# New instruction lists and PSUM banks for all five engines of a two-layer transformer kernel

## The chip, the core and the metric

The kernel runs on one core of one Trainium2 chip. A core has five engines that run their own instruction lists at the same time: PE (TensorE, matmuls), DVE (VectorE), ACT (ScalarE), POOL (GpSimd) and SP (SyncE, which here only starts DMAs). They meet through semaphores alone. The metric is the device time of one execution in microseconds (us); lower is better.

## What is computed

Two pre-norm transformer layers on `x` of 8 x 512 x 128 in float32. Each layer is attention and then a mixture of experts, each with a layernorm before it and a residual around it. Cut to its core:

```
x = x + attn0(layernorm(x))   # 16 heads of 8, 4 kv heads, causal softmax, @ wo.T
x = x + ffn0(layernorm(x))    # softmax over 8 experts, the best one: (silu(a) * g) @ w2[e], [a, g] = x @ w1[e], times its probability
x = x + attn1(layernorm(x))   # 16 heads of 8, k and v out of a normed latent of 32, rope on q and k, causal
x = x + ffn1(layernorm(x))    # softmax over 8 experts, the best two: relu(x @ w1[e] + b1[e]) @ w2[e] + b2[e], times their probabilities
```

## The kernel before

**Steps.** The function `all_steps` breaks the work into steps that carry a kind, a layer, a batch or group, and two numbers. Each step is a handful of instructions on one engine or on several. The kinds that matter here, in the order of one batch:

- Attention: `turn` (L1145, PE turns the normed rows), `lat`, `lat_turn`, `v1`, `rotate` (layer 1: latent, keys, values, rope), `park` and `stacks` (SP moves keys and queries into stacks), `max` (PE L1213 and L1219 compute scores for the row maximum, DVE L1524 reduces them to `neg_max`), `m_hi` (PE L1227 turns `neg_max`), `score` (PE L1239, then ACT L1453 takes the exponential and POOL L1088 masks), `values` (PE L1257), `normalise` (DVE L1637 and L1521 make `ctx_n`; PE L1267), `turn_ctx` (PE L1275), `project` (PE L1283).
- Routing: `logits` (PE L1292), `route` and `choose` (DVE, ACT), `places` (PE L1300 and L1301, then a chain of small DVE operations that count each token's place in its expert's rows), `scatter` (POOL L1099, an indirect DMA that puts the rows of a token block into `sorted_in`).
- Experts: `fetch` (SP L972 and L976, sorted rows into `rows_in`, two buffers), `turn_rows` (PE L1308), `fetch_w1` (SP L943, one load of weights for each tile of 128 rows, a ring of six in layer 1), `first` (PE L1331, ACT L1490), `second` (PE L1341, DVE L1521), and then in layer 0 a store to `sorted_out` and `combine` (POOL gathers, DVE L1797 adds to X), in layer 1 `send` (POOL L1107, an indirect DMA to `returned`), `take_back` (SP L997, two DMAs for a batch), `add` (DVE L1555, ACT L1499, POOL) and `store` (SP L1007). `tail` (SP L952) fills the ends of the last half's experts with empty rows. `load_expert` (SP L917) brings weights of the second matmul.

**Groups.** Layer 0 routes in two groups of four batches. Layer 1 has group 0 (batches 0 to 3, the first half) and groups 1, 2 and 3 (batches 4 and 5, 6, 7: the second half). The expert work of a group is mixed into the attention of later batches where there is any; the last burst of expert work runs from about 780 us to the end.

**What sets the order.** Nothing is scheduled at run time. `ORDERS` holds one string for each engine, one letter for each step in which the engine takes part; `Plan.read_orders` turns letters to steps, the n-th letter of a kind being its n-th step. Each engine then runs `for s in plan.order(...)` and waits, at each instruction, on the semaphore that says its input is there or its buffer free. So an instruction that waits holds all that stands behind it in its engine's list. `BANKS` gives, in the order of PE's list, the PSUM bank of each step that takes one: one digit each, with large steps on a pair of banks. Before, only the digits 0, 2, 4, 6 and 7 stand in it. A step waits until the last user of its bank has been read (`room(u)`).

**Rules that the change's steps touch.** `take_back` of a half starts with a wait for all its sends:

```
if x == rooms(1, g)[0]:
    for slot, value in enumerate(sends_made(of_half(1, half_of(1, g))[-1])):
        sp.wait_ge(sent_back[slot], value)
```

`fetch_w1` number n of layer 1 waits until the matmuls of `second` number n-6 have been read from PSUM. `fetch` number q waits for `turn_rows` number q-2. POOL puts a small operation and a wait for it (`pause`, L1032) after every second indirect DMA.

## Time and profile before

| what | value |
| --- | --- |
| runs, us | 958.96, 962.04, 961.92; median 961.92 |
| the profiled execution, us | 958.88, of it 957.0 between first and last instruction |
| granted TensorE clock, mean | 0.963 |
| PE busy | 856.2 us (89%) |
| DVE, ACT, POOL busy | 669.4, 609.4, 533.2 us |
| moved by DMA | 141.14 MB, mean 147 GB/s |

One execution was profiled. A line of the profile gives the start, the length, the engine, the line of the source, the tile written and the tiles read, and in brackets the idle time ahead of it with what ended it. `PE 89%` is an average: there are stretches of attention, in which PE and DVE are both nearly full, and bursts of expert work, in which DVE has little to do. A granted clock of 1.00 is TensorE at its full 2.4 GHz, 0.50 at 1.2 GHz. An `SPq` line is a stretch in which SP issued DMAs, their waits in it.

### The profile page before, as it was taken

What the parts mean: (1) busy time and instruction counts of PE and PEld (TensorE: products, weight loads), DVE (VectorE), ACT (ScalarE), POOL (GpSimd) and SP (SyncE); (2) the same over time, 40 slices, a digit from 0 to 9 for tenths busy, and PEclk for the clock granted to TensorE, in tenths of its full rate; (3) what the DMA queues carried; (4) which work ended last, traced back from release to release, by engine and by line L of the source; (5) the groups of instructions that cost most, each with busy time, mean ns of one, the idle gap of its engine ahead of it and who ended that gap; (6) DMA issues with size and microseconds to landing.
All of it is one profiled execution on the core that took longest, in us unless ns stands there. A gap on an engine that the chain in (4) does not pass through costs nothing.

```text
span 957.0 us, 24622 instructions
## 1 busy us (share of the span) xinstructions
PE 856.2 (89%) x8968; PEld 572.6 (60%) x8968; DVE 669.4 (70%) x1379; ACT 609.4 (64%) x1173; POOL 533.2 (56%) x809
## 2 busy tenths in 40 slices
PE   3689999989999899988999999999799997899991
PEld 1334455434999445434998444454445597799990
DVE  1889899788545899887567899789999537111117
ACT  3077889865444588685434696788578864555661
POOL 3043544557000588677203787567788775687452
PEclk9999999989999899979999999799899999999996
DMA  5625642444674436341984517435441256778786
GB/s 142 155 83 128 172 112 75 74 113 148 197 223 147 118 113 156 87 135 54 304 255 129 130 54 160 128 78 120 122 124 36 77 167 184 227 228 252 237 247 207
DMA packets 137312, 141.14 MB, mean 147 GB/s; under 512 B 35564, under 2 KB 113452, under 8 KB 137100
## 3 DMA queue, kind: packets, MB, share of 16 engines
q1 hardware_dynamic: 130604, 126.04, 47.4%
q0 software_dynamic: 6592, 13.55, 4.4%
q8 instruction: 74, 1.21, 0.5%
q14 instruction: 42, 0.34, 0.1%
HBM read 98.73 MB, written 44.36 MB: 150 GB/s over the span
## 4 chain that ended last, share of the span: by engine, by line
PE 36%; DVE 9%; issue 3%; DMA 2%; ACT 2%; SPq 0%; POOL 0%; DVEq 0%; ACTq 0%; POOLq 0%
PE psum L1331 11%; PE psum L1341 9%; PE psum L1257 5%; DVE neg_max L1524 4%; PE psum L1239 2%; PE psum L1213 2%; DMA rows_in<-sorted_in 1%; ACT scratch L1453 1%; PE psum L1308 1%; PE psum L1219 1%; PE psum L1283 1%; DVE route L1521 1%; PE psum L1175 1%; DVE X L1555 1%; DMA w<-sorted_out,rows_of 1%
## 5 line engine op out<-in xcount | busy, mean ns | idle before, releaser
L1524 DVE TENSOR_REDUCE neg_max<-psum 128x2 f32<-128x768 f32 (+3 forms) x352 | 379.6, 1119 | 41.0 <-PE psum L1219 38.7
L1453 ACT ACTIVATE scratch<-psum 128x1024 f32<-128x1024 f32 x320 | 316.1, 1022 | 80.4 <-PE psum L1239 77.9
L1088 POOL TENSOR_SCALAR_AFFINE_SELECT scratch<-scratch 128x512 f32<-128x512 f32 x256 | 158.5, 641 | 124.3 <-ACT scratch L1453 123.2
L1331 PE MATMUL psum<-rows_t,w_now 128*128 128x128 f32 x1360 | 169.5, 277 | 5.9 <-issue 3.8
L1257 PE MATMUL psum<-scratch,values 128*32 128x512 f32 (+3 forms) x2048 | 170.0, 452 | 1.7 <-POOL scratch L1088 0.8
L1331 PEld LDWEIGHTS psum<-rows_t,w_now 128*128 128x128 f32 x1360 | 159.7, 193 | 10.4 <-issue 7.4
L1213 PE MATMUL psum<-k_stack,q_stack 52*128 52x128 bf16 (+3 forms) x1024 | 133.2, 321 | 17.8 <-DVE neg_max L1524 7.9
L1341 PE MATMUL psum<-w,hidden_t 128*128 x992 | 131.3, 279 | 5.1 <-ACT hidden_t L1490 1.7
L1239 PE MATMUL psum<-q_stack,k_stack 55*128 55x512 bf16 (+3 forms) x1024 | 121.9, 312 | 12.7 <-DVE neg_max L1524 7.1
L1490 ACT ACTIVATE hidden_t<-psum,w_now 128x128 f32<-128x128 f32 x312 | 88.6, 373 | 60.6 <-PE psum L1331 46.3
L1341 PEld LDWEIGHTS psum<-w,hidden_t 128*128 128x128 f32 x992 | 119.7, 193 | 10.2 <-issue 10.0
L1099 POOL DMA_INDIRECT sorted_in<-xn_half,rows_of x96 | 94.1, 980 | 33.4 <-issue 20.8
L1213 PEld LDWEIGHTS psum<-k_stack,q_stack 52*128 52x128 bf16 x1024 | 43.8, 98 | 96.1 <-issue 39.0
L1521 DVE TENSOR_TENSOR w<-psum,w_now 128x128 f32<-128x128 f32 x78 | 22.7, 291 | 109.1 <-PE psum L1341 107.8
L1107 POOL DMA_INDIRECT returned<-w,goes_to x78 | 76.8, 985 | 37.9 <-issue 19.0
L1219 PE MATMUL psum<-masks_bf 64*128 64x64 bf16 (+2 forms) x1408 | 93.0, 211 | 0.0
L1257 PEld LDWEIGHTS psum<-scratch,values 128*32 128x32 f32 x2048 | 55.1, 111 | 62.1 <-issue 40.6
L1219 PEld LDWEIGHTS psum<-masks_bf 64*128 64x128 bf16 x1408 | 70.6, 101 | 30.9 <-issue 4.9
L1239 PEld LDWEIGHTS psum<-q_stack,k_stack 55*128 55x128 bf16 x1024 | 36.4, 96 | 73.1 <-issue 31.7
L1778 DVE SCALAR_TENSOR_TENSOR hidden_t<-w,psum 128x512 f32<-128x512 f32 x46 | 31.6, 687 | 58.2 <-PE psum L1341 33.0
L1070 POOL TENSOR_TENSOR rot<-rot 128x512 f32<-128x512 f32 x16 | 20.4, 1272 | 50.0 <-DVE rot L1521 49.9
L1078 POOL TENSOR_TENSOR max_parts<-max_rest,max_parts 32x128 bf16<-32x128 f32 x32 | 13.5, 422 | 57.3 <-ACT max_parts L1349 57.1
(141 smaller groups left out, 1007.2 us busy)
## 6 DMA issues: line engine op xcount, KB each, us to landing
w_now<-in_w SPq DMA_DIRECT2D x78, 322.0 KB
w_now<-in_w SPq DMA_DIRECT2D x46, 512.0 KB, 4.4
q_stack<-q_parts SPq DMA_DIRECT2D x64, 192.0 KB, 4.2
q_parts<-q_parts SPq DMA_DIRECT2D x16, 384.0 KB, 2.9
k_stack<-k_parts SPq DMA_DIRECT2D x32, 192.0 KB, 3.7
q_parts<-q_parts SPq DMA_DIRECT2D x16, 256.0 KB, 2.9
w<-in_w SPq DMA_DIRECT2D x16, 256.0 KB, 4.4
scratch<-returned SPq DMA_DIRECT2D x16, 256.0 KB, 4.0
```

Source lines behind the costliest of these rows:

```text
L1088: pool.affine_select(out=diag, in_=diag, compare_op=ALU.is_ge, fill=0.0, base=0, pattern=[[0, 4], [1, P]], channel_multiplier=-1).then_inc ...
L1099: pool.indirect_dma_start(sorted_in[s.layer][half_of(s.layer, g)][:, :], bass.IndirectOffsetOnAxis(ap=row_of(s.layer, g, t, k), axis=0), x ...
L1107: pool.indirect_dma_start(returned[h][:, :], bass.IndirectOffsetOnAxis(ap=goes_to[h][:, j:j + 1], axis=0), kept[slot], None).then_inc(sent ...
L1213: pe.matmul(out[:, j * width:(j + 1) * width], q_stack[i][rows, pair, t * P:(t + 1) * P], k_stack[i][rows, k_of(layer, pair), 0:width], st ...
L1219: ins = pe.matmul(blocks, ident_of[half, :], mask[half, :].unsqueeze(1).to_broadcast([P // 2, n, P // 2]), start=False, stop=(first > widt ...
L1239: ins = pe.matmul(bank[u.bank + k][:, off:off + SEQ - j * P], k_stack[i][rows, k_of(layer, pair), j * P:(j + 1) * P], q_stack[i][rows, pai ...
L1257: ins = pe.matmul(bank[u.bank][CW * c:CW * c + CW, j * P:SEQ], values[batch_of(s) % 3][:, j, col:col + CW], p[:, c % 2, off:off + SEQ - j ...
L1331: ins = pe.matmul(bank[v.bank][:, c * P:(c + 1) * P], w1_now[layer][w.slot][:, n * FFN + c * P:n * FFN + (c + 1) * P], rows)
L1341: ins = pe.matmul(bank[u.bank][:, 0:P], hidden_t[h.slot][:, k * P:(k + 1) * P], w2[layer][:, bass.ds(e, 1), k * DIM:(k + 1) * DIM].rearran ...
L1453: act.activation(expd[s.slot], psum[:, u.bank:u.bank + 2, :], ACT.Exp, scale=SCALE).then_inc(read[u.bank], 1)
L1490: ins = act.activation(hidden_t[s.slot][:, c * P:(c + 1) * P], bank[u.bank][:, c * P:(c + 1) * P], ACT.Relu, bias=w[:, FFN + c:FFN + c + 1])
L1524: return dve.tensor_reduce(out=out, in_=in_, axis=AX, op=op, negate=negate)
```

## The change

The strings of `ORDERS` are replaced for all five engines, and so is `BANKS`, in which 1, 3 and 5 now stand too. The steps are the same and so is the work of each. Since a `rotate` step can now stand ahead of its batch's `lat` step on PE, it gets the wait for the turned rows that `lat` already has. Of the strings the first row of two of them is shown.

```
 ORDERS = {
     "pe": (
-        "&ef&efjjjjjjjjjjjjjljjjjjjjjppppppjjlj&jjpepprjjjfpjjrppjrjpjljjrpj&jpjtjrpjprjjpejpjpjrjjprjpjltpjppjjujfpjvpjplrpjprpp&rjpjejjrp"
+        "&ef&&efjjjjjjjjjjjjljjjjjjjjppjppjjjppjlejjjrpprjpjfjprjrpjj&jpljppjjjjrtpjppjjrjjpejprpjjrjjp&tppjjjuljpfjpvppjrjlpprpjprjjepjrp"
...
 BANKS = (
-    "6767670240240240240624024024020204207260426027042604240240260420642074620420472404204202467024024607246024670240264026402407427024"
+    "7767675024602460246502640264026042062406540265020264026026402562042605426026026042060206245026407624704624072604024026042407247024"
...
                 elif s.kind == "rotate":
+                    x = of("turn", 1, b, "xn")
+                    pe.wait_ge(read[x.uses[0].bank], x.uses[0].after)
                     room(u)
                     pe.matmul(bank[u.bank], (wq1, wq1_sw)[s.y][:, :], xt[of("turn", 1, b, "xn").slot][:, :]).then_inc(full[u.bank], 1)
```

Two lines are added to the program, so that a line of the kernel stands two lines further down from there on (L1227 is L1229, L1797 is L1799, L1524 is L1526), except on SP and POOL, whose code stands ahead of it. Three places, as the lists have them.

**DVE, where the first burst of layer 0 has ended (318 to 327 us).** The reductions are those of batch 6, `ctx_n` is the context of batch 5, and L1797 adds a gathered block of the first group's expert output to X. Before:

```order
L1524 TENSOR_REDUCE neg_max<-psum 128x2 x6
L1797 SCALAR_TENSOR_TENSOR X<-w_1,gate,X 128x128
L1524 TENSOR_REDUCE neg_max<-psum 128x2
L1797 SCALAR_TENSOR_TENSOR X<-w_1,gate,X 128x128
L1637 RECIPROCAL ctx_rec<-psum 128x32
L1521 TENSOR_TENSOR ctx_n<-psum,ctx_rec 128x4x64
L1797 SCALAR_TENSOR_TENSOR X<-w_1,gate,X 128x128
L1524 TENSOR_REDUCE neg_max<-psum 128x2
```

After:

```order
L1526 TENSOR_REDUCE neg_max<-psum 128x2 x4
L1639 RECIPROCAL ctx_rec<-psum 128x32
L1523 TENSOR_TENSOR ctx_n<-psum,ctx_rec 128x4x64
L1526 TENSOR_REDUCE neg_max<-psum 128x2 x3
L1639 RECIPROCAL ctx_rec<-psum 128x32
L1523 TENSOR_TENSOR ctx_n<-psum,ctx_rec 128x4x64
L1526 TENSOR_REDUCE neg_max<-psum 128x2
L1799 SCALAR_TENSOR_TENSOR X<-w_1,gate,X 128x128 x2
L1523 TENSOR_TENSOR max_rest<-psum,max_parts 32x128
```

The additions that wait for a gather now stand behind all reductions of these heads and behind the normalisation of batch 5.

**PE, ahead of the transposition of `neg_max` of batch 5 in layer 1 (674 to 680 us).** Before:

```order
L1257 MATMUL psum<-scratch,values 32x512 x4
L1257 MATMUL psum<-scratch,values 32x384 x4
L1257 MATMUL psum<-scratch,values 32x256 x4
L1257 MATMUL psum<-scratch,values 32x128 x4
L1239 MATMUL psum<-q_stack,k_stack 128x384 x2
L1239 MATMUL psum<-q_stack,k_stack 128x128 x2
L1213 MATMUL psum<-k_stack,q_stack 128x128 x8
L1219 MATMUL psum<-masks_bf 128x4x64 x4
L1227 MATMUL psum<-consts,neg_max 32x128
L1213 MATMUL psum<-k_stack,q_stack 128x256 x4
```

After:

```order
L1259 MATMUL psum<-scratch,values 32x512 x4
L1259 MATMUL psum<-scratch,values 32x384 x4
L1259 MATMUL psum<-scratch,values 32x256 x4
L1259 MATMUL psum<-scratch,values 32x128 x4
L1215 MATMUL psum<-k_stack,q_stack 128x512 x2
L1221 MATMUL psum<-masks_bf 128x64 x4
L1259 MATMUL psum<-scratch,values 32x512 x4
L1215 MATMUL psum<-k_stack,q_stack 128x128 x8
L1221 MATMUL psum<-masks_bf 128x4x64 x4
L1215 MATMUL psum<-k_stack,q_stack 128x256 x4
L1221 MATMUL psum<-masks_bf 128x2x64 x4
L1229 MATMUL psum<-consts,neg_max 32x128
```

A `values` step of 512 columns and the `max` step of 128x256 now stand ahead of the transposition; a `v1` step (L1198, eight matmuls) stands some ten rows further up, where before it stood well behind.

**SP, at the take-backs of the first half of layer 1.** Before they stand next to the last loads of weights, with the second half's behind them:

```order
L943 ISA
L943 DMA w_now<-in_w_1 128x644
L997 DMA scratch<-returned 128x512 x2
L810 TENSOR_LOAD expert_of
L943 ISA
L943 DMA w_now<-in_w_1 128x644
L943 ISA
L943 DMA w_now<-in_w_1 128x644
L997 DMA scratch<-returned 128x512 x14
L1007 DMA out<-X 128x4x128 x8
```

After, three of the first half's four batches (six DMAs) are taken back right behind the last load of group 1:

```order
L943 ISA
L943 DMA w_now<-in_w_1 128x644
L810 TENSOR_LOAD expert_of
L943 ISA
L943 DMA w_now<-in_w_1 128x644
L997 DMA scratch<-returned 128x512 x6
L810 TENSOR_LOAD expert_of
L943 ISA
L943 DMA w_now<-in_w_1 128x644
L943 ISA
L943 DMA w_now<-in_w_1 128x644
```

They moved from behind 28 of the 30 loads of weights of groups 2 and 3 to a place ahead of all 30, and the first of them waits for all sends of the first half. On DVE the first three additions (L1555) of these batches moved to stand right behind the fifth of group 1's nine `second` steps, where before they followed the last but one of group 3.

Other moves that the prediction speaks of: SP issues the first six fetches of group 0's rows in layer 1 in a row and then the seventh load of weights, where before loads and fetches alternate; the eight `load_expert` steps of layer 1 are spread among the stacks of batches 5 to 7, where before they stand in two clusters; POOL sends tiles back between the scatters of batches 6 and 7, where before those sixteen scatters stand in a row but for one send; and all additions of the first half stand inside the last burst, where before all but one follow it.

## Rows read from the trace of the kernel before

**Rows 1.** Page, part 1: busy time, share and instructions.

```profile
PE 856.2 (89%) x8968; PEld 572.6 (60%) x8968; DVE 669.4 (70%) x1379; ACT 609.4 (64%) x1173; POOL 533.2 (56%) x809
```

**Rows 2.** Stretches at half clock: busy us of PE, PEld, DVE, ACT, POOL; clock, DMA share, GB/s.

```profile
323.10:329.90 6.80, 5.06 (x29) 1.83 (x29) 5.89 (x17) 2.91 (x4) 3.90 (x8) 0.50 0.23 53
...
603.00:613.20 10.20, 10.20 (x59) 5.87 (x59) 6.74 (x7) 7.16 (x15) 6.41 (x10) 0.50 0.33 93
678.00:684.90 6.90, 5.41 (x41) 3.39 (x43) 6.59 (x10) 2.72 (x5) 4.32 (x7) 0.51 0.48 141
...
835.10:838.50 3.40, 3.40 (x18) 3.40 (x18) 0.00 (x0) 2.12 (x8) 2.75 (x5) 0.50 1.03 345
sum 54.70, PE 48.84 PEld 23.62 DVE 43.29 ACT 32.75 POOL 38.89; mean PE 5.43 PEld 2.62 DVE 4.81 ACT 3.64 POOL 4.32
```

**Rows 3.** Waits of PE: for whom, total us, times, longest.

```profile
PE psum L1145 <- ACT xn L1412: 13.0, 2, 11.0
PE psum L1213 <- DVE neg_max L1524: 7.9, 22, 1.0
```

**Rows 4.** Timeline of DVE, 320 to 324: start, length, operation, idle before it.

```profile
320.45 0.41 DVE L1797 SCALAR_TENSOR_TENSOR X<-w,gate,X 128x128 f32<-128x128 f32 x1 [1.59 <-DMA w<-sorted_out,rows_of]
...
323.44 0.53 DVE L1797 SCALAR_TENSOR_TENSOR X<-w,gate,X 128x128 f32<-128x128 f32 x1 [1.43 <-DMA w<-sorted_out,rows_of]
```

**Rows 5.** Timeline of PE, 322 to 325.

```profile
322.06 0.39 PE L1213 MATMUL psum<-k_stack,q_stack 52*128 52x512 bf16 x2 [1.05 <-DVE neg_max L1524]
...
324.84 1.09 PE L1275 MATMUL psum<-consts,ctx_n 128*128 128x128 f32 x4 [2.33 <-DVE ctx_n L1521]
```

**Rows 6.** Timeline of PE, 668 to 680.

```profile
668.88 1.07 PE L1257 MATMUL psum<-scratch,values 128*32 128x512 f32 x8
...
679.49 0.40 PE L1227 MATMUL psum<-consts,neg_max 128*32 128x128 f32 x1 [3.47 <-DVE neg_max L1524]
679.82 0.61 PE L1213 MATMUL psum<-k_stack,q_stack 52*128 52x256 bf16 x4
```

**Rows 7.** Timeline of DVE, 670 to 681.

```profile
670.28 0.40 DVE L1719 TENSOR_TENSOR_SCAN route<-consts,psum 128x128 f32<-128x128 f32 x1
...
678.23 2.34 DVE L1524 TENSOR_REDUCE neg_max<-psum 128x2 f32<-128x1024 f32 x2
```

**Rows 8.** Timeline of PE, 412.9.

```profile
412.93 0.29 PE L1300 MATMUL psum<-chosen,masks_bf 128*128 128x128 bf16 x1 [2.33 <-DVE chosen L1696]
```

**Rows 9.** Two stretches of the last burst, columns as in rows 2.

```profile
786.00:812.00 26.00, 20.36 (x166) 18.68 (x165) 19.76 (x102) 12.20 (x42) 17.32 (x24) 1.00 0.63 185
...
864.00:934.00 70.00, 67.70 (x590) 66.15 (x589) 11.53 (x42) 43.40 (x149) 41.63 (x60) 1.00 0.81 246
```

**Rows 10.** Timeline of SP, 791 to 830.

```profile
791.71 7.80 SPq L943 DMA_DIRECT2D w_now<-in_w  x2
799.61 0.39 SPq L976 DMA_DIRECT2D rows_in<-sorted_in  x1
...
819.89 10.20 SPq L952 DMA_DIRECT2D sorted_in<-in_empty_rows  x8
```

**Rows 11.** Timeline of PE, 833.8 and 935.1, its last matmuls.

```profile
833.78 2.65 PE L1331 MATMUL psum<-rows_t,w_now 128*128 128x128 f32 x16 [3.00 <-issue]
...
935.11 1.15 PE L1341 MATMUL psum<-w,hidden_t 128*128 x8 [0.42 <-ACT hidden_t L1490]
```

**Rows 12.** Timeline of POOL, 814 to 866.

```profile
814.32 0.96 POOL L1099 DMA_INDIRECT sorted_in<-xn_half,rows_of  x1 [6.87 <-DVE xn_half L1546]
...
830.07 1.00 POOL L1099 DMA_INDIRECT sorted_in<-xn_half,rows_of  x1 [3.93 <-DVE xn_half L1546]
...
865.89 0.96 POOL L1107 DMA_INDIRECT returned<-w,goes_to  x1 [0.30 <-issue]
```

**Rows 13.** Source line L997, take_back: durations in ns, first and last start; landing.

```profile
L997 SPq DMA_DIRECT2D scratch<-returned x16: 320/426/1455, 923.4 to 945.9; - x16
...
DMA to landing us min/median/max: 2.6/4.0/5.8
```

More of the change, by code:

```diff
@@ new lines @@
+    "pool": (
+        "bbggbggmppppmpbpggbpppmppppgppmpbppgppmppppgpbppmpgppbpbppmpppgpmppbpppgpppmpppbpbmgpppppppp44gp44p4p4m444444p44p44ppppgmgbpmppppp"
+        "GGGGppGpGbGpmGbpbppcJpKGgppmJbKppgGpGpbbmpGcGpJGpKpgpppGJGpppmbKgbbpcbmppJpppp55K5g55p55p55p5m5p5p55J55bpKppgJcKpbgmJKgppGGpGGGpGm"
+        "pGbpGppGGpGbGbppmJGpKcGppGgbJpKgbmppppGpbcJKppbgmbpJppKpgbpmpJpcpKppgppJpmKppgpbbppmpcJpKgpppppJpK44m4p4p4g44p44p44m4pp4p4p44bp4p4"
+        "mp444ppp44pb4p4p4mp4pp44p4mp4p4ppppb55pp55p5p5p555555558885b8888686668888688887688888885886688777888888878878889977999999+9++++++-"
+        "+---------------------SS"),
@@ new lines @@
+    "2462540207246270470246046204024607246027402240340620247062047026470624720426040624024602476042704625027403044271436024760247026470"
+    "2460247042402640024602540624072604702402460246024604720472074260246204304202704627042062407264702020470241240246343642162462406240"
+    "2604621024602506026064206240264027426042604260420420462760274062407264206406024027460724702403406024760627656254540767627640762754"
+    "0347675702677605247675075027676760276560454241706743042404345260627607767065265067277606542575076276076276077277670772776")
@@ L1173, in _ @@
                 elif s.kind == "rotate":
+                    x = of("turn", 1, b, "xn")
+                    pe.wait_ge(read[x.uses[0].bank], x.uses[0].after)
                     room(u)
```

71 lines of the change are left out of this document (31 added, 40 removed).

## The prediction

> **What bounds the kernel now.** I read the page first. PE is busy for 856.2 of 957.0 us and DVE for 669.4 [rows 1]. The work of every step stays as it is, so the change can only touch two things: the 101 us in which PE stands idle, and the time in which PE works at a low clock. Of the idle time 11.0 us lie before the first matmul [rows 3] and 20.7 us behind the last one, which ends at 936.3 [rows 11]; both are latency of loads and stores. That leaves about 69 us for waits inside. The stretches at half clock are nine, 54.70 us together, in which PE is busy for 48.84 [rows 2]. The same work at full clock would take half as long, so they hold at most 24 us. Ahead of most of them stands a wait of PE of 0.8 to 3.5 us.
>
> Then the waits of PE by cause. Most are small: 22 waits for `neg_max` ahead of L1213 make 7.9 us, none above 1.0 [rows 3]. These are waits of the PSUM bank, in stretches where DVE and PE are both nearly full. A few are long, and for these the timelines of PE and of the engine waited for show what stood ahead of the late operation. An order can mend just that. So the working goes by the long waits, against the profiled execution of 958.88 us, which lies 3.04 us under the median of 961.92.
>
> **Part 1, the end of layer 0's first burst.** PE waits 1.05 and 2.33 us [rows 5]. DVE had come late twice, since it stood in additions that waited 1.59 and 1.43 us for a gather, ahead of a reduction and of the normalisation that makes `ctx_n` [rows 4]. The new DVE list puts these additions behind both. Idle to be had: 1.05 + 2.33 = 3.38 us. The half-clock stretch at 323.1 has 5.06 us of PE work [rows 2], so up to 2.5 more if it goes. The ends are 0 and -5.9; I take -4, since nothing late is left in front of `ctx_n`, while I can't say that the clock stays up.
>
> **Part 2, `m_hi` of batch 5 in layer 1.** PE waits 3.47 us [rows 6] for a reduction that starts at 678.23, behind the chain of `places`, which DVE runs from 670.28 on [rows 7]. DVE's list keeps that order. PE's puts three steps of work ahead of the wait: a `values` step of 512 columns (1.07 us by its row), the `max` step (0.61 at half clock, so 0.3), and `v1`, which has no row; it is eight matmuls, as the `values` step's row has, of fewer columns, so at most 1.07 [rows 6]. That makes 2.4 us of cover, and about 1 us of wait stays. Half clock holds 5.41 us of PE work here [rows 2], up to 2.7 to be had, but waits of about 1 us stand before other such stretches, so I take only 0.6 of it: -3, ends 0 and -6.2.
>
> **Part 3, `places` at 412.9.** The wait is 2.33 us [rows 8]; the new list has a turn of the latent and a score in front of it, together under the 1.07 us of the `values` step. -0.8, ends 0 and -1.1.
>
> **Part 4, the seam of attention and last burst.** From 786 to 812 us PE is busy 20.36 of 26.00 us, so 5.6 are idle, at full clock [rows 9]. SP starts the fetch of the sixth set of rows at 799.61, behind two loads of weights that hold it for 7.80 us while they wait for room in the ring [rows 10]. Now six fetches stand together, ahead of the seventh load. The sixth has to wait for the fourth `turn_rows`, and that load behind it; between this step and the `first` that needs the load lie seven PE steps, some 7 us, so the load is covered. -3, ends 0 and -5.6.
>
> **Part 5, smaller ones.** The `load_expert` DMAs, once a cluster ahead of the 10.2 us at half clock from 603.0 [rows 2], are spread: -2, ends +1 and -5. `tail` holds SP 10.20 us [rows 10] and PE then waits 3.00 us for weights [rows 11], with 3.40 us at half clock behind it; `tail` stays at the same place with half a us more of cover: -0.5. At the end DVE's additions of the first half are gone from the way of the second's, whose last take-back starts at 945.9 and lands 4.0 us later [rows 13]; that landing still sets the end: -1. Start: `load_rest` is put off and the loads of x come earlier, 0 within 1. The added wait in `rotate` costs nothing: the turned rows were read many steps before.
>
> **Part 6, what the take-backs cost.** Six DMAs with a median of 0.43 us on SP [rows 13] now stand ahead of the first load for group 2. They wait for all sends of the first half. Before, the last of them is issued at 865.89 [rows 12], while SP would be ready at about 867. POOL had come to that point late because it had stood idle 6.87 and 3.93 us ahead of scatters with sends behind them [rows 12]; the new list has sends between the scatters, so that POOL should have them out by 860. Then SP passes on with 6 x 0.43 = 2.6 us. PE has some nine steps until it needs the load; 67.70 us with 590 matmuls, eight a step [rows 9], make 0.92 us a step, 8 us of cover. Against it stand 2.6 us on SP, a load's own landing (2.6 to 5.8, as those of take_back [rows 13]) and the 1.5 MB of the six in front of it: at the 345 GB/s of the busiest stretch [rows 2] 4.4 us. The need is 5 to 13 us against 8: a stall of 0 to 5. In addition DVE's first addition stands behind the fifth `second` of group 1, and the sixth can't be read until the take-back has landed. I take +4 for both, ends 0 and +9.
>
> That the six DMAs' bytes pass first is visible here only in part: the DMA share in this stretch is 0.81 [rows 9], so there is room, but little. The Trainium skill, "DMA: Bandwidth & Descriptors", section "Queues, rings and completion order", says that on each DMA engine the descriptors of a queue are consumed in ring order. By that rule loads of weights wait for the whole 1.5 MB, and the stall is nearer to 5 than to 0; without it the loads would share, and it would be nearer to 0. No row here decides it.
>
> **Part 7, waits that the new lists bring.** Every row of every list is new, and the small waits will lie elsewhere. As many may go as come; but long ones come without being seen from the lists. The long ones of before are 3.47, 3.00, 2.33 and 2.33; one and a half new ones of this kind, 2.8 each, make +4. Ends -4 and +12. The new banks 1, 3 and 5 are in this: they can shorten the 7.9 us of rows 3, or move them.
>
> **Sum.** -4 - 3 - 0.8 - 3 - 2 - 0.5 - 1 = -14.3; +4 + 4; together -6.3. 958.88 - 6.3 = 952.6, and on the median's scale 952.6 + 3.04 = 955.6, so 955.5.
>
> **Rivals.**
>
> *The waits move and don't go.* In attention DVE is busy for 5.89 of 6.80 and 6.59 of 6.90 us around parts 1 and 2 [rows 2]. If DVE is the real bound there, what PE doesn't wait at these places it waits a few steps on. Parts 1, 2 and 3 then give -2 in place of -7.8: 955.5 + 5.8 = 961.3, no change. For it: the chain of `places` isn't shortened. Against it: part 1 takes waits for a DMA off DVE itself, which is a true gain for DVE.
>
> *The take-backs block SP: slower.* The place is the load of weights behind the six DMAs. If POOL's sends are as late as before (865.89), or PE gets there earlier by what the other parts give, SP stands from its arrival until the last send has landed, some 2.6 to 5.8 us after issue. The point from which it decides: SP arrives more than 1 us before that landing. If SP arrives at 860 and the last send lands at 868 to 871, SP stands 8 to 11 us, PE 9 to 13 in all, with a half-clock stretch of 1.7 more. With 5 to 9 us over the +4 already taken, and with parts 1 and 2 giving half, the time is 955.5 + 7 + 3.5 = 966. For it: POOL sends two tiles in 2.65 us and was late by a dozen us before. Against it: the idle 10.8 us of POOL that the new list can use.
>
> *All goes.* The half-clock stretches of parts 1 and 2 go too (-2 and -2), the spread loads give -5, take-backs cost 1: 955.5 - 4 - 3 - 3 = 945.5.
>
> That the change doesn't do what it says can't be: the lists are what the engines run.
>
> **How the numbers follow.** Forecast (950 to 959): 0.42. Waits move (959 to 964.8): 0.19. Blocked and slower (above 964.8): 0.27. All goes (below 950): 0.12. A measurement of this kernel tells a difference of about 0.3%, 2.9 us, from none. Faster is below 959.0: 0.42 + 0.12 = 0.54; same 0.19; slower 0.27. The range of 8 in 10 leaves out about a tenth at either side: the middle of the last case, 943, and the upper part of the blocked case, 968.
>
> **What would show it.** Part 1: no addition with a wait for a gather between the reductions near 320, and L1275 without a wait above 1 us. Part 2: the wait ahead of the transposition of `neg_max` of batch 5 at about 1 us, and the clock in the 7 us behind it. Part 4: idle time of PE in the first 26 us of the last burst below 3 us. Part 6: the length of the stretch in which SP issues the six take-backs; near 3 us the forecast holds, near 10 us the rival does, and PE would show a wait by issue ahead of L1331. The total is wrong from the root if PE's idle time inside stays near 69 us, or if the stretches at half clock sum to more than 60 us. What I can't see from here is part 7, and it is the largest doubt.

## The result

The changed kernel is slower. Its median over 20 runs is 973.76 us (967.65 to 979.19), against 959.18 us (957.25 to 970.73) for 20 runs of the kernel before in the same comparison. The ratio is 1.0134, with a 95% interval of 1.0107 to 1.0161. I had forecast 955.5 and a range of 943 to 968. The profiled execution took 976.56 us, 974.7 of them between first and last instruction, with a mean granted clock of 0.946 instead of 0.963.

First the page of the changed kernel: busy time by engine, and the chain that ended last.

```profile
PE 855.6 (88%) x8968; PEld 575.5 (59%) x8968; DVE 668.5 (69%) x1379; ACT 606.8 (62%) x1173; POOL 531.9 (55%) x802
...
PE 45%; DVE 13%; POOL 11%; DMA 11%; issue 8%; SPq 7%; ACT 5%; DVEq 0%; POOLq 0%; ACTq 0%
```

PE is busy for as long as before [rows 1], so the 17.7 us that the span grew are time without work. PE's first matmul waits 10.9 us and its last ends at 953.8, 20.9 us from the end, both as before. What is left is 974.7 - 855.6 - 10.9 - 20.9 = 87.3 us of idle time inside, against 69.1 by the same sum for before. In the chain of the changed kernel DMA has 11% and SP's queue 7%. The chain of before could be followed back only to 454 us, so its shares can't be set beside these.

The waits of PE in the changed kernel, by cause: total us, times, longest.

```profile
PE psum L1241 <- DMA q_stack<-max_parts_out: 13.4, 9, 3.0
PE psum L1333 <- DMA w_now<-in_w: 13.2, 8, 4.0
PE psum L1215 <- DVE neg_max L1526: 9.2, 23, 0.7
...
PE psum L1215 <- DMA q_stack<-q_parts: 4.0, 1, 4.0
```

The waits for the PSUM bank (L1215 for `neg_max`) are close to what they were, 9.2 against 7.9 us [rows 3]. New are 30.6 us of waits for DMAs, none of which before has: for the row maxima and queries of a stack (13.4 and 4.0), and for weights (13.2).

Where it went in time shows when one subtracts the start times of the same PE step in the two traces, changed minus before:

| PE step | at (before), us | changed | difference |
| --- | --- | --- | --- |
| tile 18 of layer 0's first burst | 293.2 | 295.6 | +2.4 |
| projection of batch 5, layer 0 | 330.6 | 326.6 | -4.0 |
| turn of batch 7's half, layer 0 | 404.3 | 403.2 | -1.1 |
| projection of batch 0, layer 1 | 450.1 | 454.8 | +4.7 |
| turn of batch 1's context, layer 1 | 557.5 | 562.3 | +4.8 |
| projection of batch 2, layer 1 | 609.2 | 607.7 | -1.5 |
| turn of batch 3's half | 655.5 | 653.8 | -1.7 |
| projection of batch 4 | 694.1 | 697.0 | +2.9 |
| tile 0 of group 1, last burst | 855.6 | 861.0 | +5.4 |
| tile 18 of group 3 | 926.5 | 944.6 | +18.2 |

So at 855 us the gains and losses leave a loss of 5.4 us, and the other 12.8 us are lost behind it. These are numbers of one trace each. Run e1 below has the lists of the changed kernel up to 870 us, and its trace differs from this one by up to 2.6 us at the steps ahead of 700 us and by 3.5 us at 855.6, where it has +1.9. So a small entry of the table says little, and of the loss at 855 us it isn't sure how much is there.

That last stretch in the changed kernel: SP with the take-backs (L997), then POOL with its last send of the first half (the 39th send; the first half has 39 tiles), DVE's first additions (L1557) and PE's two waits for weights.

```profile
871.04 2.71 SPq L997 DMA_DIRECT2D scratch<-returned  x6
874.87 0.94 SPq L943 DMA_DIRECT2D w_now<-in_w  x2
878.64 4.91 SPq L972 DMA_DIRECT2D rows_in<-sorted_in  x8
...
894.49 1.74 SPq L997 DMA_DIRECT2D scratch<-returned  x2
897.39 5.30 SPq L972 DMA_DIRECT2D rows_in<-sorted_in  x8
902.88 8.91 SPq L943 DMA_DIRECT2D w_now<-in_w  x5
```

```profile
865.26 1.00 POOL L1107 DMA_INDIRECT returned<-w,goes_to  x1 [0.55 <-issue]
```

```profile
877.79 3.43 DVE L1557 SCALAR_TENSOR_TENSOR X<-scratch,gate,X 128x128 f32<-128x128 f32 x12 [3.75 <-DMA scratch<-returned]
```

```profile
881.77 2.05 PE L1333 MATMUL psum<-rows_t,w_now 128*128 128x128 f32 x8 [4.04 <-DMA w_now<-in_w]
...
906.33 2.08 PE L1333 MATMUL psum<-rows_t,w_now 128*128 128x128 f32 x8 [4.01 <-DMA w_now<-in_w]
```

The last send is issued at 865.26, not by 860 as I had worked out, and the first take-back goes out at 871.04. Yet SP did not stand for the sends. Its last load ends at 870.01, and the sixteen waits that it has ahead of the take-backs pass one after the other in 0.03 us each, until 871.00. The load for group 2 follows at 874.87 and PE gets its weights at 881.77. In both of PE's waits a stretch at half clock begins. Busy us of PE, PEld, DVE, ACT and POOL, then clock, DMA share and GB/s:

```profile
880.40:887.20 6.80, 5.43 (x25) 5.46 (x26) 1.58 (x8) 1.58 (x5) 2.35 (x4) 0.50 0.72 205
904.30:911.10 6.80, 4.77 (x22) 4.77 (x23) 0.09 (x1) 0.03 (x1) 0.11 (x1) 0.50 0.63 198
426.40:443.50 17.10, 16.24 (x113) 8.15 (x111) 8.33 (x10) 5.73 (x9) 14.76 (x19) 0.50 0.19 54
668.80:679.00 10.20, 9.88 (x66) 4.34 (x70) 7.88 (x23) 6.03 (x7) 5.00 (x8) 0.50 0.40 78
```

Part 4 of my sum, in contrast, came as forecast. From 786 to 812 us PE is now busy for 22.99 of 26.00 us, where it was 20.36 [rows 9]:

```profile
786.00:812.00 26.00, 22.99 (x199) 22.02 (x197) 16.75 (x82) 15.53 (x52) 21.22 (x31) 1.00 0.66 196
```

### The profile page after: what moved, and what is told of

It is laid out like the page before. It is cut to its first block, busy times and chain, and to the rows that moved or that the text cites. A ratio compares the mean times of both kernels' runs of the same rounds, so it can differ in the third digit from the quotient of the medians.

```text
span 974.7 us, 24668 instructions
## 1 busy us (share of the span) xinstructions
PE 855.6 (88%) x8968; PEld 575.5 (59%) x8968; DVE 668.5 (69%) x1379; ACT 606.8 (62%) x1173; POOL 531.9 (55%) x802
## 4 chain that ended last, share of the span: by engine, by line
PE 45%; DVE 13%; POOL 11%; DMA 11%; issue 8%; SPq 7%; ACT 5%; DVEq 0%; POOLq 0%; ACTq 0%
PE psum L1333 11%; PE psum L1259 8%; PE psum L1343 7%; DVE neg_max L1526 6%; PE psum L1215 4%; PE psum L1241 4%; POOL sorted_in L1099 3%; ACT scratch L1455 3%; POOL scratch L1088 3%; DMA w_now<-in_w 2%; DMA max_parts_out<-max_parts 2%; DMA q_stack<-max_parts_out 2%; POOL w L1117 1%; PE psum L1221 1%; PE psum L1285 1%
## 5 line engine op out<-in xcount | busy, mean ns | idle before, releaser
L1526 DVE TENSOR_REDUCE neg_max<-psum 128x2 f32<-128x768 f32 (+3 forms) x352 | 378.2, 1118 | 54.6 <-PE psum L1221 52.9
L1333 PE MATMUL psum<-rows_t,w_now 128*128 128x128 f32 x1360 | 173.0, 281 | 19.1 <-DMA w_now<-in_w 13.2
L1333 PEld LDWEIGHTS psum<-rows_t,w_now 128*128 128x128 f32 x1360 | 163.1, 196 | 23.5 <-DMA w_now<-in_w 10.7
L1215 PE MATMUL psum<-k_stack,q_stack 52*128 52x128 bf16 (+3 forms) x1024 | 128.6, 311 | 23.4 <-DVE neg_max L1526 9.2
L1241 PE MATMUL psum<-q_stack,k_stack 55*128 55x512 bf16 (+3 forms) x1024 | 120.2, 313 | 24.2 <-DMA q_stack<-max_parts_out 13.4
L1215 PEld LDWEIGHTS psum<-k_stack,q_stack 52*128 52x128 bf16 x1024 | 42.5, 96 | 88.9 <-DVE neg_max L1526 28.3
L1523 DVE TENSOR_TENSOR w<-psum,w_now 128x128 f32<-128x128 f32 x78 | 22.1, 289 | 102.7 <-PE psum L1343 102.7
L1221 PE MATMUL psum<-masks_bf 64*128 64x64 bf16 (+2 forms) x1408 | 90.2, 206 | 0.0
L1241 PEld LDWEIGHTS psum<-q_stack,k_stack 55*128 55x128 bf16 x1024 | 36.5, 96 | 88.0 <-issue 27.4
L1483 ACT ACTIVATE w<-psum 128x512 f32<-128x512 f32 x46 | 27.4, 595 | 37.4 <-PE psum L1333 27.6
L1046 POOL TENSOR_TENSOR ln_small<-ln_small,consts 128x4 f32<-128x4 f32 x40 | 41.4, 1035 | 3.1
```

Source lines behind the costliest of these rows:

```text
L1215: pe.matmul(out[:, j * width:(j + 1) * width], q_stack[i][rows, pair, t * P:(t + 1) * P], k_stack[i][rows, k_of(layer, pair), 0:width], st ...
L1221: ins = pe.matmul(blocks, ident_of[half, :], mask[half, :].unsqueeze(1).to_broadcast([P // 2, n, P // 2]), start=False, stop=(first > widt ...
L1241: ins = pe.matmul(bank[u.bank + k][:, off:off + SEQ - j * P], k_stack[i][rows, k_of(layer, pair), j * P:(j + 1) * P], q_stack[i][rows, pai ...
L1333: ins = pe.matmul(bank[v.bank][:, c * P:(c + 1) * P], w1_now[layer][w.slot][:, n * FFN + c * P:n * FFN + (c + 1) * P], rows)
L1526: return dve.tensor_reduce(out=out, in_=in_, axis=AX, op=op, negate=negate)
```

## The experiments

**A second thing turned up on the way.** The kernel before takes 959 to 961 us on some chips and 1041 to 1052 us on others (two chips gave the one time, two the other, with no overlap over 13 to 23 runs each). On the slow ones the profile of every kernel has waits that no kernel had in the first comparison. Their releaser is named `remote`. These are from c3, the kernel before with one edit: total us, times, longest.

```profile
DVE w L1521 <- remote: 38.0, 5, 15.9
...
ACT hidden_t L1490 <- remote: 32.5, 5, 12.4
```

ACT and DVE wait there for a semaphore that PE raises, and PE is long done. One such place in c3: PE's `first` matmuls (L1331), ACT that takes their result, and POOL, which sends rows all the while.

```profile
902.13 1.06 PE L1331 MATMUL psum<-rows_t,w_now 128*128 128x128 f32 x8
907.17 1.28 PE L1341 MATMUL psum<-w,hidden_t 128*128 x8 [3.98 <-issue]
```

```profile
915.15 1.14 ACT L1490 ACTIVATE hidden_t<-psum,w_now 128x128 f32<-128x128 f32 x4 [12.42 <-remote]
```

```profile
914.59 0.96 POOL L1107 DMA_INDIRECT returned<-w,goes_to  x1 [0.30 <-issue]
...
917.25 0.96 POOL L1107 DMA_INDIRECT returned<-w,goes_to  x1 [0.30 <-issue]
```

From the semaphore events of the traces one can take the time from a matmul's start to its increment. Here the last matmul of the row at 902.13 starts at 902.9 and its increment comes at 915.1. For L1341 the time is 0.29 us for 122 of 124 steps in the trace of before, near an indirect DMA and elsewhere alike. In c3 it is 0.29 us for 55 of the 58 steps that have no indirect DMA within 1.5 us, and 0.43 for the other three; of the 66 nearer ones only 35 have 0.29, and 30 of the other 31 have 0.33 to 5.42 us. So on some chips TensorE's increments come late while POOL issues indirect DMAs. Such chips are called late ones below, the others punctual. The first comparison was made on a punctual one, by its time for the kernel before and by its two traces, which have no such wait, and so were e, g and h.

| run | kernel | before there | ratio (95% interval) | chip |
| --- | --- | --- | --- | --- |
| c1 | changed, take-backs late | 1041.32 | 0.9706 (0.9644 to 0.9768) | late |
| c2 | before, take-backs early | 1041.32 | 1.0067 (1.0032 to 1.0102) | late |
| c3 | before, gathers' additions later | 1041.32 | 0.9980 (0.9954 to 1.0007) | late |
| c4 | changed to 350 us, then before | 1041.32 | 0.9930 (0.9892 to 0.9967) | late |
| d1 | changed | 1050.43 | 0.9770 (0.9699 to 0.9841) | late |
| d2 | as c1 | 1050.43 | 0.9654 (0.9583 to 0.9724) | late |
| d3 | changed, additions alone late | 1050.43 | 0.9699 (0.9631 to 0.9767) | late |
| d4 | changed to 350 and from 560 to 640 us | 1050.43 | 0.9921 (0.9882 to 0.9960) | late |
| e1 | as c1 | 960.97 | 1.0058 (1.0024 to 1.0092) | punctual |
| e2 | as c2 | 960.97 | 1.0047 (1.0014 to 1.0081) | punctual |
| f1 | as c3 | 1051.56 | 0.9994 (0.9954 to 1.0035) | late |
| f2 | before, 560 to 640 us of changed | 1051.56 | 0.9978 (0.9940 to 1.0016) | late |
| f3 | as c4 | 1051.56 | 0.9927 (0.9883 to 0.9971) | late |
| f4 | changed, one POOL step later | 1051.56 | one run, 1029.59 us | late |
| g1 | as c3 | 959.57 | 1.0003 (0.9969 to 1.0037) | punctual |
| g2 | as f2 | 959.57 | 1.0001 (0.9978 to 1.0024) | punctual |
| h1 | before, all four additions later | 959.60 | 1.0038 (1.0007 to 1.0069) | punctual |
| h2 | h1 and g2 together | 959.60 | 1.0009 (0.9976 to 1.0041) | punctual |

### The take-backs

The edit of c1, d2 and e1: in the changed kernel the letters of `take_back` (R), `store` (> ! ? .) and `add` (* / = <) go back to where they stood, counted by weight loads (D) on SP and by `second` steps (F) on DVE.

```
 "sp":
-  ...DDDBBDDDBDDDDDDDRRRDDBBDDDDDDDRBBDDDDDBDDDDBDDDDDDDDD>DD>>>DRRRR!!?.
+  ...DDDBBDDDBDDDDDDDDDBBDDDDDDDBBDDDDDBDDDDBDDDDDDDDDDRDDRRRRRRR>>>>!!?.
 "dve":
-  ...BFFFFFBFFFFF***FFFBFFFFFBFFBFF*FF**FF*BB*FFFFBFFFFFFFFFFFFFF//=<=<
+  ...BFFFFFBFFFFFFFFBFFFFFBFFBFFFFFFBBFFFFBFFFFFFFFFFFFF*F*******//==<<
```

c2 and e2 are the reverse, made in the kernel before:

```
 "sp":
-  ...DDDDDDBDDBDDDDBDDDDDBDDDDDDBDDBDDDBDDDBDDDBDDDDDDDRDDRRRRRRR>>>>!!?.
+  ...DDDDDDBDDBDDDDBDRRRDDDDBDDDDDRDBDDBDDDBDDDBDDDBDDDDDD>DD>>>DRRRR!!?.
 "dve":
-  ...FBFFFFBFFFFBFFFFFBFFFFFBFFFBFFFBFFBFFFBFFFFFFFFFFFF*F*******//==<<
+  ...FBFFFFBFFFF***BFFFFFBFFFFFBFF*FBF**FF**BFFBFFFBFFFFFFFFFFFFF//=<=<
```

What was expected of c1, c2, d1 and d2:

> The changed kernel, but the take-backs and stores (SP) and the additions (DVE) of the first half stand where the kernel before has them. Theory 1 (the take-backs inside the burst cost the time: SP waits for the last send, loads of weights come late, twice a PE wait of 4 us with half clock behind it): the 14 us lost behind 855 us come back but for 1 or 2, so about 961 to 963 us, within 0.5% of before. Rival (the burst is late for another reason, such as scatters that POOL now does later or rows fetched later): above 968 us, both 4 us waits at L1333 still there.

> The kernel before, with only the take-backs and stores (SP) and the additions (DVE) of the first half put where the changed kernel has them, by count of weight loads and of second steps. Theory 1: slower by 8 to 14 us (967 to 973 us), with two new waits of PE for weights of 3 to 4 us near 875 and 900 us. Rival: within 3 us of before.

> The changed kernel as it is, beside the next three on one chip, as their reference. Where ScalarE and VectorE don't stand for long on a queue the profile can't name: 1.0% to 1.6% slower than before, as measured first. Theory: the two PE waits of 4 us for weights behind the take-backs are there again.

> Again the changed kernel with take-backs, stores and additions of the first half at the place of before. Theory 1 (take-backs cost 8 to 12 us): faster than the changed kernel by 8 to 12 us. Rival (the changed burst loses the time without them): by less than 4 us.

c1 and d1 missed their numbers, which were worked out for a punctual chip. On a late one the changed kernel is *faster* than before by 2.3%, and with late take-backs by 2.9 and 3.5%. The median of d2 is 9.1 us under that of d1 on the same chip (1014.77 against 1023.85), as theory 1 wants, but with four runs each, whose times overlap, this pair alone is not clear of the noise. Of the two 4 us waits of d1's expectation one was there, 4.27 us at 946.34; in place of the other stood 1.79 us at 923.32. c2 lost 6.7 us (8 to 14 expected), which is clear of the noise, with one wait for weights of 5.62 us in place of two.

e1 and e2 repeated it where the increments are punctual:

> The changed kernel with take-backs, stores and additions of the first half late, once more. In the runs so far VectorE and ScalarE stood for some 110 to 130 us on a releaser that the profile names remote, near the indirect DMAs; the traces of the first comparison show none of it. If this chip shows none: 960 to 966 us, at most 0.6% slower than before (take-backs cost 8 to 12 of the 14.6 us that were lost). If it shows it: 3% faster than before, as twice measured.

> The kernel before with the early take-backs, stores and additions, once more. Without the remote waits: 6 to 10 us slower than before, two waits of PE for weights of 3 to 4 us each behind 870 us. With them: 0.7% slower, as measured. Rival (without them SP isn't late and nothing is lost): within 3 us of before.

e1 came out at 966.8 us, 0.58% above before, where the changed kernel is 1.34% above. Against before the take-backs thus cost 1.34 - 0.58 = 0.76%, 7.3 us (the two intervals make that 3 to 11), and 5.6 us of the loss are something else. e2 took 966.26, a loss of 0.47%, 4.5 us, below the 6 to 10 expected. Instead of two waits it shows one, at the load right behind the six DMAs. SP, DVE and PE in e2:

```profile
869.22 2.87 SPq L997 DMA_DIRECT2D scratch<-returned  x6
873.28 7.45 SPq L943 DMA_DIRECT2D w_now<-in_w  x4
```

```profile
874.03 3.43 DVE L1555 SCALAR_TENSOR_TENSOR X<-scratch,gate,X 128x128 f32<-128x128 f32 x12 [4.87 <-DMA scratch<-returned]
```

```profile
879.49 2.05 PE L1331 MATMUL psum<-rows_t,w_now 128*128 128x128 f32 x8 [5.30 <-DMA w_now<-in_w]
```

The mechanism stands alone in e2: 5.30 us of waiting by one edit. At the `first` step of 871.4 us e2 is 0.8 us behind before, at that of 876.5 us 7.1, and at the last one 7.9. The second wait of the changed kernel is of another make-up. It stands behind a take-back and eight row fetches in a row (5.30 us of SP at 897.39), and in e1, with the take-backs gone, PE still waits twice for weights here, though shorter:

```profile
881.33 2.05 PE L1333 MATMUL psum<-rows_t,w_now 128*128 128x128 f32 x16 [1.66 <-DMA w_now<-in_w]
...
896.27 1.16 PE L1333 MATMUL psum<-rows_t,w_now 128*128 128x128 f32 x8 [1.95 <-DMA w_now<-in_w]
```

Each of the two stands right behind eight row fetches in a row. SP in e1, and then in before, which issues four at a time and has no wait of PE for weights:

```profile
872.65 4.93 SPq L972 DMA_DIRECT2D rows_in<-sorted_in  x8
877.81 8.70 SPq L943 DMA_DIRECT2D w_now<-in_w  x7
887.77 4.94 SPq L972 DMA_DIRECT2D rows_in<-sorted_in  x8
892.89 7.02 SPq L943 DMA_DIRECT2D w_now<-in_w  x5
```

```profile
886.29 1.88 SPq L972 DMA_DIRECT2D rows_in<-sorted_in  x4
```

This is also where e1 falls behind: it is 0.5 us ahead of before at the `first` step of 867.9 us and 5.1 behind at that of 914.9. So the fetches in pairs are the likely cause of most of the other 5.6 us, but no run changed them alone. A rival is the clock. The mean granted clock over e1's ten runs is 0.949, where before has 0.961 on that chip and e2 0.959, so a lower clock goes with the rest of the changed lists and not with the take-backs. The profiled run of e1, at 0.960, shows little of it.

d3 parted SP's share from DVE's. Its edit is that of d2 without moving R:

> The changed kernel with its early take-backs on SP, but with the additions (DVE) and stores of the first half at the place of before. It parts two costs of the early take-backs. If SP's queue and the DMAs' bytes do the harm (SP waits for the last send, loads of weights stand behind 1.5 MB): within 2 us of the changed kernel, both 4 us waits there. If VectorE's additions do it (they hold the reads of PSUM and by them the ring of weights): faster by 6 us or more, and the second wait gone at least.

It took 1018.25 us: 5.6 us less than d1 and 3.5 more than d2. With four runs each, whose times spread over 4 to 15 us, neither difference is clear of the noise. The trace says more. If the additions on DVE did the harm, the second wait was to be gone; it is there, 4.82 us at 949.04, with the additions out of the way. So the second wait is made by SP's queue. In place of the first, PE waits 1.04 us for issue and 0.53 for weights. What share of the time the additions have stays open.

### The first place: additions that wait for a gather

c3, f1 and g1 change one thing in the DVE list of before. G is an addition of gathered rows (L1797), j a reduction (L1524), t the normalisation. h1 takes all four additions behind.

```
 "dve": at the end of layer 0's first burst
-  GjGtGjG
+  jtGGGjG      (c3, f1, g1)
+  jtjGGGG      (h1)
```

> The kernel before, on DVE alone: the first two additions of gathered rows near 320 us stand behind the reduction and the normalisation of batch 5. Part 1 of the prediction: the waits of 1.05 and 2.33 us at PE go, 4 to 6 us faster than before (953 to 955). Rival (DVE is the bound there and PE waits a few steps on): within 1.5 us of before.

> The kernel before with the two additions of gathered rows on DVE behind the reduction and the normalisation of batch 5, once more, for a chip without the remote waits. Part 1 of the prediction: 2 to 4 us faster (both waits near 322 us go; half clock may stay). Rival (DVE is the bound, PE waits further on): within 1 us.

> As f1, in case this chip shows no remote waits: 2 to 4 us faster than before by part 1 of the prediction; within 1 us by the rival. In the two runs with remote waits the long waits near the place went, yet PE's milestones behind it moved by 0.

> The kernel before; on DVE all four additions of gathered rows near 320 us stand behind both reductions and the normalisation, as the changed list has it. In g1, with three of the four ahead of the last reduction, ctx_n came 3.2 us earlier but the last reduction came late and PE waited 2.75 us ahead of L1227. If that was the misplaced reduction: this wait goes and PE's milestones near 334 us are 2 to 4 us ahead of before. If DVE has no time to give: 0, with a new wait elsewhere by 350 us.

c3 and f1, on late chips, gave 0.998 and 0.9994: no gain. g1, on a punctual one, gave 1.0003, and its trace shows why. PE in g1:

```profile
321.66 0.66 PE L1275 MATMUL psum<-consts,ctx_n 128*128 128x128 f32 x4
...
326.03 0.28 PE L1227 MATMUL psum<-consts,neg_max 128*32 128x128 f32 x1 [2.75 <-DVE neg_max L1524]
```

The turn of the context, L1275, has lost its wait of 2.33 us [rows 5] and comes 3.2 us earlier, just as part 1 says. Then PE waits 2.75 us for the last reduction, which DVE does after additions that still wait for their gathers:

```profile
324.49 0.35 DVE L1797 SCALAR_TENSOR_TENSOR X<-w,gate,X 128x128 f32<-128x128 f32 x1 [0.49 <-DMA w<-sorted_out,rows_of]
324.75 1.22 DVE L1524 TENSOR_REDUCE neg_max<-psum 128x2 f32<-128x1024 f32 x1
```

h1 took that reduction out of the way too, as the changed kernel does. The wait went again, and came again one step on. PE in h1:

```profile
326.08 1.83 PE L1257 MATMUL psum<-scratch,values 128*32 128x512 f32 x8 [2.79 <-DVE logits L1521]
```

This is a `values` step that wants the bank of the routing logits, and DVE reads the logits only behind the fourth addition. PE was 1.3 us ahead of before at 334 us. Then h1 lost it, and more: by 375 us it was 3.1 us *behind*. At 367 us the same kind of wait comes a third time. PE and DVE in h1:

```profile
367.34 0.61 PE L1239 MATMUL psum<-q_stack,k_stack 55*128 55x512 bf16 x2 [2.00 <-DVE neg_max L1524]
```

```profile
365.79 0.35 DVE L1797 SCALAR_TENSOR_TENSOR X<-w,gate,X 128x128 f32<-128x128 f32 x1 [2.22 <-DMA w<-sorted_out,rows_of]
```

The reduction stands behind this addition. In before the addition has no wait, though its gather is issued at 359.27, 0.3 us later than in h1; from 360 to 365 us the DMA engines are busy for 0.98 of the time in h1 and 0.79 in before. The clock differs too. In h1:

```profile
350.10:353.60 3.50, 3.50 (x32) 1.24 (x32) 1.97 (x3) 1.59 (x3) 3.27 (x6) 0.51 0.45 145
367.20:370.60 3.40, 3.26 (x17) 2.25 (x19) 1.69 (x12) 0.47 (x3) 2.20 (x5) 0.50 0.32 72
```

In before the first of these stretches runs at full clock:

```profile
350.10:353.60 3.50, 3.50 (x44) 2.11 (x46) 3.09 (x6) 1.97 (x5) 3.34 (x7) 1.00 0.06 14
```

At 361 us h1 is still 0.2 us ahead; 1.1 us are lost by then, with the first stretch and no wait above 0.37 us. The 3.3 us behind it hold the wait of 2.00 us and the second stretch. g1 has both stretches and a wait of 1.22 us at the same place. No run held the clock and changed only the order, so the share of each is not shown. h1 as a whole is 0.38% slower than before.

### Stretches of the changed order in the kernel before

c4 and f3 take, on every engine, the changed kernel's order for all it starts before 350 us, and the order of before for the rest. f2 and g2 do it for 560 to 640 us, d4 for both, h2 is g2 with the edit of h1. PE's banks go with its steps. The edit in words of the lists:

```
 for each engine:
-  list of before
+  list of changed up to 350 us, then the steps still missing in the order of before   (c4, f3)
+  before to 560 us, missing steps of changed to 640 us, then missing steps of before   (f2, g2)
```

> Lists and banks of all engines as in the changed kernel for all steps that it starts in its first 350 us, and from there on in the order of the kernel before. Against before, the changed kernel has steps of 330 us some 4 us earlier. If gains and losses of the stretches simply add: 3 to 4 us faster than before (955 to 957). Rival (a lead is eaten by DVE or DMA waits further on): within 1.5 us of before.

> The changed kernel's order to 350 us, then that of before. By the milestones of the two traces without remote waits: 1 to 2 us faster than before, within what can be measured. With remote waits: 0.7% faster, as measured.

> The lists of the kernel before, but with the order of the changed one in two stretches in which its trace gained: all engines up to 350 us, and from 560 to 640 us. If stretches add: 3 us from the first and 4 to 5 from the second, 6 to 9 us faster than before. Rival (leads are eaten further on): within 3 us of before.

> The kernel before, with all engines in the order of the changed kernel from 560 to 640 us. In the trace of the changed kernel this stretch takes 5 to 8 us less (the half-clock stretch of 10.2 us at 603 is gone and the loads of expert weights are spread). If stretches add: 4 to 7 us faster than before. Rival (what is won is given back by 680 us): within 2 us.

> As f2, in case this chip shows no remote waits. In f2 PE was 9 us ahead at the output projection of batch 2 and had given all but 4 us back when batch 3 was normed. By that: 2 to 4 us faster than before here. If the stretch adds as in the changed kernel's trace: 6 us or more.

> h1 together with the order of the changed kernel from 560 to 640 us. Without remote waits: 2 to 4 us of the first and 1 of the second, 3 to 5 us faster than before (0.3 to 0.5%), the best that the parts of the change have to give by these runs. If leads are eaten: within 2 us.

On late chips c4 and f3 gave 0.7% twice; this start was not run on a punctual one. d4, with the second stretch added, gave 0.8%, so the second added nothing that can be told. f2 and g2, at 0.9978 and 1.0001, show no gain by themselves either, and the trace of g2 tells what becomes of one. At the projection of batch 2 PE is 7.1 us ahead of before, at the turn of batch 3's half only 1.4. At the seam between the two orders come a half-clock stretch and these waits (PE in g2):

```profile
636.45 0.61 PE L1241 MATMUL psum<-q_stack,k_stack 55*128 55x512 bf16 x2 [1.58 <-DVE rot L1523]
...
647.53 0.39 PE L1241 MATMUL psum<-q_stack,k_stack 55*128 55x512 bf16 x2 [1.90 <-DMA q_stack<-max_parts_out]
```

The 7 us are thus partly work put off. h2 came to 1.0009 (960.34 us). None of the mixtures that ran on a punctual chip beats the kernel before.

### Why the routing chain near 410 us got longer

In the changed kernel DVE's subtraction on two SBUF tensors (L1523, `route` and `consts`) takes 4.13 us, where the nine others of its kind take 0.2 to 0.6. DVE and then POOL in the changed kernel:

```profile
408.82 4.13 DVE L1523 TENSOR_TENSOR route<-route,consts 128x128 f32<-128x128 f32 x1
```

```profile
409.18 1.80 POOL L1088 TENSOR_SCALAR_AFFINE_SELECT scratch<-scratch 128x512 f32<-128x512 f32 x3
410.96 1.26 POOL L1070 TENSOR_TENSOR rot<-rot 128x512 f32<-128x512 f32 x1
412.18 0.62 POOL L1088 TENSOR_SCALAR_AFFINE_SELECT scratch<-scratch 128x512 f32<-128x512 f32 x1
```

It ends at 412.95, with the end of POOL's row of work at 412.80. f4 puts one POOL step later, so that POOL has a gap:

```
 "pool": sum of the rotated q parts (J), masks (p)
-  ppJp
+  pppJ
```

> The changed kernel; on POOL alone the addition of the rotated q parts of batch 2 in layer 1 (L1070) moves behind the next mask. In the changed kernel a VectorE operation on two 128x128 SBUF tensors takes 4.13 us at 408.8 instead of 0.29, to the end of a row of POOL operations without a gap. If POOL's SBUF work shuts it out: it ends where POOL first idles now, after 2.0 to 2.5 us. If it is something else (its own input late): 4.1 us again.

DVE and POOL in f4:

```profile
417.46 2.31 DVE L1523 TENSOR_TENSOR route<-route,consts 128x128 f32<-128x128 f32 x1
```

```profile
417.81 1.80 POOL L1088 TENSOR_SCALAR_AFFINE_SELECT scratch<-scratch 128x512 f32<-128x512 f32 x3
419.97 0.64 POOL L1088 TENSOR_SCALAR_AFFINE_SELECT scratch<-scratch 128x512 f32<-128x512 f32 x1 [0.35 <-ACT scratch L1455]
```

The operation ends at 419.77, in POOL's gap of 0.35 us, after 2.31 us. Before has a shorter case in the same chain, an operation that elsewhere takes 0.2 us. DVE in before:

```profile
409.27 1.64 DVE L1521 TENSOR_TENSOR gate<-route_small 128x16 f32<-128x16 f32 x1
```

It ends at 410.91, and POOL's row of work at 410.88. Of the time of the whole kernel the one run of f4 tells nothing: 1029.59 us, where the changed kernel has 1023.85 on another late chip. So POOL's work in SBUF shuts a DVE operation with two SBUF inputs out. That is what the Trainium skill says in "SBUF — State Buffer", section "SBUF: two separate sides": an exclusive lock, and the loser fully blocks; here it blocks over a row of POOL instructions, until POOL pauses. In the changed kernel the operation took 3.8 us longer than alone. The chain from the logits to `chosen` took 8.25 us, against 5.83 in before, so 2.4 us more. In f4 it is 7.7, since two later operations stand there instead (0.63 and 1.38 us). The cover that PE got at `places` left 0.86 us of wait.

## Why the prediction was wrong, point by point

**The step that failed is the one from the length of a wait to a gain, in parts 2 and 3 above all and in part 1.** All terms but part 6 and the -1 at the end lie ahead of tile 0 of group 1 (855.6 us in before), and sum to -9.3. Measured there is +5.4, and +1.9 in e1, which has the same lists up to that point. So 11 to 15 of the 21 us between forecast and measurement are gains priced by what a wait or a stretch of before could give at its own place, with the rest of the order thought away, and the kernel didn't keep them: parts 2 and 3 read +4.6 and +5.8 where I had -3 and -0.8. Behind that point I had +3, and it became +12.8. This is part 6, with a second place of waiting that I hadn't seen.

**Part 6: the mechanism held, its size did not.** I had POOL's last send by 860. It was at 865.26, since the `second` step that feeds it came at 862.8 us on PE, 5.0 us later than in before; POOL's gained time could not help there. But the blocked case, by which SP stands 8 to 11 us for the send, did not happen, for SP's waits passed at once. What happened is the sum of this part itself. From 870.01, when SP is ready, to 881.77, when PE has its weights, are 11.8 us, inside my 5 to 13: 4.9 on SP (I had 2.6) and 6.9 for the landing. PE had 7.7 us of cover (I had 8), and so waited 4.04. Two things I had at nothing: the half clock that comes with the wait (6.8 us, with 5.43 us of PE's work in it), and the second place, 4.01 us at 906.33 with half clock once more. My sign for this part was badly chosen. The stretch with the six take-backs is 2.71 us long, near the 3 that was to mean that the forecast holds. The term measured 7.3 us by e1 against the first comparison, 9.1 by d2 against d1 (not clear of the noise), and 4.5 and 6.7 in the kernel before. Behind this stands the ordering rule that I cited from the Trainium skill, "DMA: Bandwidth & Descriptors", section "Queues, rings and completion order". By it the weights wait for all bytes ahead of them, and the traces agree: the last of the six take-backs lands at 880.85 and the load issued behind them at 881.67, 6.8 us after its issue, where the median load has 4.3. In e2 they land at 878.59 and 879.40. In e1 the load issued at 877.81, with no take-back ahead of it, lands after 3.5 us.

**Part 1 failed at the step from wait to gain.** The two waits are gone in the changed kernel, and L1277 stands without one. I took 4 of the 5.9 us for it "since nothing late is left in front of `ctx_n`". But behind it there was. The move alone gave nothing in four runs (0.998 to 1.004), and g1 and h1 show the wait reappear at the next two steps that stand behind the same additions. In the changed kernel, where all else moves too, PE gained 6.4 us from 293 to 331 us (from +2.4 to -4.0), and lost 2.9 of them by 404 us. That this leaves 3.5 us, close to my 4, is no proof of part 1, for no run shows which edit earned them. My first rival, with 19%, had said that the waits would move on.

**Part 2 failed in sign.** The wait of 3.47 us went, and one of 1.50 came ahead of L1241 at 669.12, ten us ahead of the old place. The stretch at half clock grew from 6.9 to 10.2 us (668.8 to 679.0), full of work. PE went from -1.7 us at 655 to +2.9 at 694. I had taken -3, it was +4.6. The clock is not all of it: in e1, with the same lists, the stretch is 3.4 us long and PE still loses 2.3 us between these steps. The rest of the cause stays open.

**Part 3 was wrong in sign.** The wait at `places` fell from 2.33 to 0.86 us, but the chain ahead of it took 2.4 us longer, beside POOL's row of work, and the half-clock stretches around and behind it are 6.8 and 17.1 us instead of 10.2 and 3.4 (10.2 and 17.1 in e1). From 404 to 450 us the changed kernel lost 5.8 us. I had priced only the cover, and not what moves on the other engines in these 50 us. What made the long stretch at half clock is not known.

**Part 4 was right** in place and size: PE's idle time in the 26 us fell by 2.6 to 3.0 (forecast a fall of 3).

**Part 5.** The 10.2 us at half clock from 603.0 are gone in the changed kernel, and between the turn of batch 1's context (+4.8) and that of batch 3's half (-1.7) it gained 6.5 us, where I had taken 2. g2 shows that most of it isn't kept by the kernel before when it goes on in its own order. The term for `tail` was neither gain nor loss that I can name; PE waits 2.01 us for issue at 833.77 and 3.11 for weights at 838.01, more than the 3.00 before.

**Part 7, the new waits,** I had put at 4 us and called the largest doubt. They are 17.4 us of waits for stack DMAs, 4.0 of them at 40.13 us, and I had not looked at SP's order of stacks against `load_rest` and `fill` closely enough. Their cost is not 17.4 us, since up to 293 us the changed kernel is only 2.4 us late.

The range was too narrow on the slow side, 968 against 973.76. I had worked out the blocked case at 966 with halved gains elsewhere, and not joined it with a gain of nothing.

## What to carry to other kernels

When an instruction that waits is moved back on its engine, follow all that stands behind it in its new place and not only what it held up: here a wait of 2.33 us came back as 2.75, and then as 2.79 us. Transfers that nothing needs yet should not stand in the queue that feeds the bound engine: six DMAs of 0.43 us each, with the additions that use them, cost 4.5 to 9 us there, though none had to wait. A trace of one execution should be set beside a second one before a difference of 2 or 3 us in it is explained. And before an order of instructions is judged, it should be timed on more than one chip.

## What the hardware showed that I had not expected

**TensorE's increments.** On the chips of c, d and f, ScalarE and VectorE stood for 105 to 137 us in sum on `remote`, up to 16.8 us at once (f3). The kernel before is 80 to 92 us slower on them (1041 to 1052 against 959 to 961). The changed order, 1.34% slower on a punctual chip, is 2.3% faster on a late one, and without the early take-backs 2.9 to 3.5% faster. Why some chips do this, no run tells. The kernels that start with the changed lists stand a little less on `remote` (105 to 124 us) than those that start with the lists of before (126 to 137), but that is not all of the difference, and why they do is open. That an increment stays late for as long as POOL's row of indirect DMAs lasts is not so: in c3 it came after 12.2 us with the row still running.

**The clock.** A half-clock stretch also came where PE had had no wait above 0.37 us for 16 us and was busy for 14.23 of 15.10 us, in h1 at 350.1 us. Over the changed kernel the stretches sum to 85.3 us before PE's last matmul, against 54.6 in before. Up to 869 us they are 71.7 us in it and 58.0 in e1, with the same lists. A long wait less is not a stretch less, and the clock of one trace is not that of the next.

**The lock.** A VectorE operation of 0.29 us took 4.13 us beside a closed row of GpSimd work and 2.31 us when that row had one gap of 0.35 us. The 4.13 us come again in all of c1, d1, d2, d3 and e1 (4.13 to 4.14).
